# A gate product in which four of eight token groups are taken as two pairs, with seven block products for eight

## The reference

```python
x = x + xattn(layernorm(x), ctx, Wq, Wkv)     # one head, softmax over 128 context rows
x = x + ffn(layernorm(x), w_gate, w_up, w_down)

def ffn(x, w_gate, w_up, w_down):             # w_gate, w_up: (1536, 512); w_down: (512, 1536)
    x = act_qdq(x)                            # 16 bit: round(x / scale) * scale, scale = max|x| / 32767
    up = act_qdq(x @ lpbq_dequant(w_up).T)    # weights: 4 bit in blocks of 32
    gate = act_qdq(x @ lpbq_dequant(w_gate).T)
    sig = fixed_qdq_u16(sigmoid(gate))
    gate = act_qdq(gate * sig)
    o = act_qdq(gate * up)
    return o @ lpbq_dequant(w_down).T
```

## Time and profile before

| | us |
|---|---|
| median of 3 runs | 903.09 (899.49 to 903.94) |
| span of the profiled execution | 898.3 |
| gate matmuls (L871), 1152 | 250.5 |
| up matmuls (L903), 1152 | 249.0 |
| TensorE busy | 865.5 |
| VectorE busy | 651.1 |
| ScalarE busy | 560.2 |
| GpSimd busy | 157.4 |

### The profile page before, as it was taken

The page is one execution under the profiler, slowest core; times in us unless marked ns, Lnnn a source line. Parts: engine busy times, 40 slices in busy tenths (PEclk is TensorE's granted clock), DMA queues, the critical chain, the costliest instruction groups (busy, mean ns, idle before and its releaser), DMA issues.

```text
span 898.3 us, 11791 instructions
## 1 busy us (share of the span) xinstructions
PE 865.5 (96%) x4144; PEld 426.7 (47%) x4144; DVE 651.1 (72%) x918; ACT 560.2 (62%) x673; POOL 157.4 (18%) x160
## 2 busy tenths in 40 slices
PE   7999969999999999999999989999799989999998
PEld 5777544444444444444444434444344434444443
DVE  4879883754346243279997859856999997999892
ACT  2378875553553454489997859763789975555430
POOL 0099940089001950000000000000000000000000
PEclk9999989999999999999999999999999999999999
DMA  9822319775369649884339993799998897989872
GB/s 347 332 93 98 128 59 305 205 194 198 140 234 296 206 161 294 322 319 157 132 149 327 363 347 142 251 402 373 374 379 265 276 322 271 386 286 406 317 294 100
DMA packets 107548, 230.20 MB, mean 256 GB/s; under 512 B 47216, under 2 KB 47216, under 8 KB 105328
## 3 DMA queue, kind: packets, MB, share of 16 engines
q1 hardware_dynamic: 106352, 225.48, 70.8%
q10 hardware_dynamic: 1152, 4.19, 1.3%
HBM read 127.40 MB, written 92.27 MB: 245 GB/s over the span
## 4 chain that ended last, share of the span: by engine, by line
PE 66%; DVE 16%; issue 8%; DMA 6%; ACT 3%; SPq 0%; POOL 0%; DVEq 0%; ACTq 0%
PE ps L871 28%; PE ps L948 13%; PE ps L903 10%; PE ps L975 3%; DVE big L1596 3%; PE ps L804 3%; DVE big L1589 3%; PE ps L743 2%; PE ps L818 2%; DVE small L1523 2%; DMA big<-gate_park 2%; DMA product_park<-big 2%; DVE small L1511 2%; DVE big L1518 1%; PE ps L965 1%
## 5 line engine op out<-in xcount | busy, mean ns | idle before, releaser
L993 ACT ACTIVATE big<-ps 128x1024 f32<-128x1024 f32 (+2 forms) x166 | 138.7, 845 | 189.6 <-PE ps L871 102.8
L871 PE MATMUL ps<-big 128*128 (+1 forms) x1152 | 250.5, 381 | 2.3 <-DVE big L1460 2.3
L903 PE MATMUL ps<-big 128*128 (+1 forms) x1152 | 249.0, 379 | 2.3 <-ACT big L993 2.3
L871 PEld LDWEIGHTS ps<-big 128*128 128x128 f16 x1152 | 113.1, 98 | 139.4 <-issue 4.6
L903 PEld LDWEIGHTS ps<-big 128*128 128x128 f16 x1152 | 112.6, 98 | 138.5 <-issue 2.8
L1478 DVE TENSOR_REDUCE small<-big 128x1 f32<-128x1024 f32 x48 | 58.3, 1219 | 135.2 <-ACT big L993 135.1
L948 PE MATMUL ps<-big 128*128 128x512 f16 x576 | 125.1, 379 | 2.7 <-DVE big L1617 2.7
L683 POOL PARTITION_ALL_REDUCE small<-small x8 | 3.3, 410 | 509.3 <-DVE small L1558 181.5
L948 PEld LDWEIGHTS ps<-big 128*128 128x128 f16 x576 | 56.2, 98 | 71.1 <-issue 2.9
L929 PE MATMUL ps<-big 128*128 128x512 f16 x384 | 85.2, 383 | 4.5 <-ACT big L1223 4.5
L1529 DVE CUSTOM_DVE_ANT_0 big<-big,small 128x1024 f32<-128x1024 int16 x48 | 61.7, 1284 | 7.3 <-ACT big L1173 0.5
(11 more groups left out here) (101 smaller groups left out, 1008.9 us busy)
## 6 DMA issues: line engine op xcount, KB each, us to landing
big<-up_park SPq DMA_DIRECT2D x90, 512.0 KB, 6.5
up_park<-big SPq DMA_DIRECT2D x48, 512.0 KB, 3.9
gate_park<-big SPq DMA_DIRECT2D x42, 512.0 KB, 2.9
big<-gate_park SPq DMA_DIRECT2D x42, 512.0 KB, 5.7
sign_park<-big SPq DMA_DIRECT2D x48, 256.0 KB, 3.1
big<-in_x_dram SPq DMA_DIRECT2D x8, 1024.0 KB, 17.5
x_park<-big SPq DMA_DIRECT2D x8, 1024.0 KB, 3.9
product_park<-big SPq DMA_DIRECT2D x16, 512.0 KB, 5.8
```

The lines of the kernel that those rows point to most:

```text
L871: mm = nc.tensor.matmul(ps[:, 2 * (n % 2) + j], w[:, a, k, o:o + P], XT[:, g, b, k], start=(k == 0 and a + b == 0), stop=(k == KC - 1 and ...
L903: mm = nc.tensor.matmul(ps[:, b + j], WU[:, a, k, o:o + P], XT[:, g, c, k], start=(k == 0 and a + c == 0), stop=(k == KC - 1 and c == 1))
L993: return nc.scalar.activation(dst, src, ACT.Copy)
```

## The change

Groups 0 to 3 are computed as before (`flat_unit`, 24 units). Groups 4 to 7 become two pairs, (6, 7) first and (4, 5) second. For a pair and one of the six channel positions (a *quad*, 12 of them) there are two token groups, two blocks of channels and two halves of the inner dimension, a 2 x 2 by 2 x 2 block product. It is done with seven block products of six matmuls, where eight would be the plain way. TensorE runs them in the order P1, P5, P4, P6, P3, P2 of the next quad, P7: the seven calls of `six` and `first_of` in `quad` below. For that

- four sums of weight blocks (`SUMS`) are made once: GpSimd adds (`first_sums`, `last_sum`, ten operations of 1536 columns), ScalarE and VectorE split them (`sum_hi`, `sum_lo`) at units 8, 10, 13 and 16; the gate weights are scaled to 256 in place of 2048 at the top, so that the sums fit;
- four sums of token blocks per pair (`turns`) are made by VectorE from the turned integers of h, and split (`turn_raw`, `turn_hi`, `turn_lo`) at units 11 to 13 for pair (4, 5) and 17 to 19 for pair (6, 7);
- the seven products go into four banks, of which two sets alternate; ScalarE copies partial results out (`copy_out`), VectorE combines them into four halves of 512 columns (`combine`), takes their maxima (`half_max`), ScalarE their signs (`half_sign`), and SP stores each half and its signs.

Around it: the turns of h for groups 6 and 7 move to units 13 to 16 and their splits to units 15 and 17. The down weights are now first: loaded at the start of the stage, split at units 14, 16, 18 and 19 (three `natural_hi` on ScalarE and three `natural_lo` on VectorE each; `natural_hi` of a chunk waits for `natural_lo` of the chunk two before, since its output lies over inputs already used), turned at units 15, 17, 19 and 21 through a single buffer and stored one unit later each (`turn_down_weights` waits for the split and for the parking before, `park_down_weights` for its turns). The up weights are loaded in four parts at units 22 and 23, their block maxima stand on VectorE behind unit 23 and in quad 0, and they are split in quads 5 to 8 and turned in quads 7 to 10. All 48 gate tiles are now stored and fetched again; the fetches of tiles 1 to 7 are issued behind the last product, those of 8 to 22 beside the first eight up units. `WD` has another order of its dimensions.

The diff, cut to its core:

```diff
-WTOP = 2048.0
+WTOP = (256.0, 2048.0, 2048.0)
+FLAT_G = 4
+FLAT = FLAT_G * UPG
+PAIRS = (NG - FLAT_G) // 2
+QUADS = PAIRS * UPG
+SUM_AT = (8, 10, 13, 16)
+SPLIT_AT = (3, 5, 7, 9, 11, 15, 17)
+DOWN_AT = (14, 16, 18, 19)
+TURN_AT = (18, 12)
+UP_AT = (5, 6, 7, 8)
...
+            for u in range(FLAT):
+                sp.wait_ge(g_ev, u + 1)
+                sp.dma_start(gate_d[u], gate_out[:, u % 2]).then_inc(g_st[u % 2], 16)
+                sp.wait_ge(sign_ev, u + 1)
+                sp.dma_start(sign_d[u], sign_out[:, u % 2]).then_inc(sign_st[u % 2], 16)
+                if u < 10:
+                    turn_half(u)
+                if 13 <= u < 17:
+                    turn_half(u - 3)
+                if u in (15, 17, 19, 21):
+                    turn_down_weights((u - 15) // 2)
+                if u in (16, 18, 20, 22):
+                    park_down_weights((u - 16) // 2)
+                if u == 22:
+                    load_up_weights(0)
+                    load_up_weights(1)
+                if u == 23:
+                    load_up_weights(2)
+                    load_up_weights(3)
...
+            def quad(q):
+                base, pr, n = 4 * ((q + 1) % 2), q // UPG, q % UPG
+                g, T = pair_group(pr), turns(pr)
+                need(pe, c_ev, C_EV + 4 * (q - 1) if q > 1 else 0)
...
+                six(base, n, WG[:, 0], XT[:, g, :, 0:2], True)
...
+                six(base + 3, n, SUMS[:, 0], T[:, 0], True)
+                six(base + 2, n, WG[:, 2], T[:, 3], True)
+                pe.wait_ge(c_ev, C_EV + 4 * q + 1)
+                six(base, n, SUMS[:, 1], T[:, 2], False)
+                pe.wait_ge(copy_ev, COPY_EV + 4 * q + 2)
+                six(base + 3, n, SUMS[:, 2], XT[:, g + 1, :, 2:4], False)
...
+                if q + 1 < QUADS:
+                    first_of(q + 1, 4 - base)
+                pe.wait_ge(copy_ev, COPY_EV + 4 * q + 4)
+                six(base, n, SUMS[:, 3], T[:, 1], False)
...
+            for u in range(FLAT):
+                act.wait_ge(g_mm, u + 1)
...
+                if u in SUM_AT:
+                    sum_hi(SUM_AT.index(u))
+                for pr in range(PAIRS):
+                    for j in range(4):
+                        if u == TURN_AT[pr] + j // 2:
+                            turn_hi(pr, j)
+                for c in range(OC):
+                    if u == DOWN_AT[c // 3]:
+                        natural_hi(2, c)
+                act.wait_ge(g_ev, u + 1)
...
+                nc.scalar.activation(sign_out[:, u % 2], gate_out[:, u % 2], ACT.Sign).then_inc(sign_ev, 1)
...
+                if u in SPLIT_AT:
...
+                    split_h(g)
...
+                if u in SUM_AT:
+                    sum_lo(SUM_AT.index(u))
+                for pr in range(PAIRS):
+                    if u == TURN_AT[pr] - 1:
+                        turn_raw(pr, 0)
+                        turn_raw(pr, 1)
+                    if u == TURN_AT[pr]:
+                        turn_lo(pr, 0)
+                        turn_lo(pr, 1)
+                        turn_raw(pr, 2)
+                        turn_raw(pr, 3)
+                    if u == TURN_AT[pr] + 1:
+                        turn_lo(pr, 2)
+                        turn_lo(pr, 3)
+                for c in range(OC):
+                    if u == DOWN_AT[c // 3]:
+                        natural_lo(2, c)
+                if u == FLAT - 1:
+                    up_block_max(0)
+                    up_block_max(1)
...
+            for q in range(QUADS):
+                base = 4 * ((q + 1) % 2)
+                if q:
+                    last_halves(q - 1)
...
+                combine(q, 0, base, copy_b, ALU.add)
+                if q:
+                    half_max(q - 1, 2)
+                    half_max(q - 1, 3)
...
+                if q == 0:
+                    up_block_max(2)
+                    up_block_max(3)
+                    block_scales(1)
...
+                half_max(q, 0)
...
+                combine(q, 1, base + 3, copy_u, ALU.add)
+                half_max(q, 1)
```

More of the change, by code:

```diff
@@ L468, in _ @@
[L468 to L479 removed]
+                                 transpose=True).then_inc(h_turn[g % 2], 16)
@@ L892, in _ @@
             gate(0)
-            with nc.tensor.Fori(1, NG) as g:
+            with nc.tensor.Fori(1, FLAT_G) as g:
                 gate(g)
-            pe.wait_ge(wu_turned, 16 * (2 * KC + H_ODD))
+            for g in range(FLAT_G, NG):
+                pe.wait_ge(hlo_d, g + KC)
+            first_of(0, 4)
+            for q in range(QUADS):
+                quad(q)
+            pe.wait_ge(wu_turned, 16 * 2 * KC)
             def raise_unit(g, n):
@@ L1140, in _ @@
[L1140 to L1147 removed]
+            for u in range(FLAT):
+                act.wait_ge(g_mm, u + 1)
+                need(act, g_mx, u - 1)
+                if u >= 2:
+                    act.wait_ge(g_st[u % 2], 16 * (u // 2))
+                copy(gate_out[:, u % 2], ps[:, 2 * (u % 2):2 * (u % 2) + 2].rearrange("p b w -> p (b w)")).then_inc(g_ev, 1)
+                if u % 2 and u < 2 * NG - 3:
+                    h_int((u + 3) // 2)
+                if u in SUM_AT:
[8 more added lines that the diff above has]
+                act.wait_ge(g_ev, u + 1)
+                if u >= 2:
+                    act.wait_ge(sign_st[u % 2], 16 * (u // 2))
+                else:
+                    act.wait_ge(hq_d, KC + 1)
+                nc.scalar.activation(sign_out[:, u % 2], gate_out[:, u % 2], ACT.Sign).then_inc(sign_ev, 1)
@@ new lines, in copy_out, with half_sign @@
+            def copy_out(dst, bank, scale=1.0):
+                nc.scalar.activation(dst, ps[:, bank], ACT.Copy, scale=scale).then_inc(copy_ev, 1)
+            def half_sign(q, x):
+                act.wait_ge(c_ev, C_EV + 4 * q + x + 1)
+                if q:
+                    act.wait_ge(cs_st[x], CS_ST + 16 * q)
+                else:
+                    act.wait_ge(sign_st[x // 2], 16 * FLAT // 2)
+                nc.scalar.activation(sign_half[:, x], gate_half[:, x], ACT.Sign).then_inc(c_sign, 1)
@@ L1471, in _ @@
             scalar2(col["fg"], col["xs"], col["pw0"], 1.0)
-            def gate_max(g, turned=None, units=range(UPG)):
-                for n in units:
-                    dve.wait_ge(g_ev, g * UPG + n + 1)
-                    kept = isinstance(g, int) and g * UPG + n >= STAY
-                    nc.vector.tensor_reduce(gcol[:, bass.ds(g * UPG + n, 1)], shelf[:, SHELF[n]] if kept else gate_out[:, n % 2],
-                                            AX.X, ALU.max, apply_absolute_value=True).then_inc(g_mx, 1)
-                    u = g * UPG + n if isinstance(g, int) else NU
-                    if u % 2 and 3 <= u < 2 * NG:
-                        split_h(u // 2)
-                    if turned is not None:
-                        for c in (range(2 * n, 2 * n + 2) if turned == 1 else range(3 * n, min(3 * n + 3, OC))):
-                            natural_lo(turned, c)
```

569 lines of the change are left out of this document (377 added, 192 removed).

## The result

| | before | after |
|---|---|---|
| median of the runs, us | 903.24 (899.49 to 903.94) | 920.23 (918.46 to 921.12) |
| span of the profiled execution, us | 898.3 | 918.8 |
| gate stage (first gate matmul to first up matmul), us | 250.3 | 266.2 |
| up stage, us | 251.3 | 255.3 |

The ratio is 1.0188, with a 95% interval of 1.0162 to 1.0213: slower, by 17.0 us where +7.3 had been forecast, and just above the range. The profiled spans differ by 20.5 us: 15.9 in the gate stage, 4.0 in the up stage, 0.6 behind it.

A forecast was written before the change was run, and what follows sets the result against it. TensorE was taken to bound the gate stage, its matmuls back to back. The terms -15.6 + 4.1 + 1.7 + 13.5 + 3.1 + 0.5 = +7.3 us on 903.1 gave 910.4 us, range 896 to 918.

The forecast's parts named there:

- Matmuls saved: Gate stage: 72 matmuls fewer at 0.2163 us each, -15.6 us.
- the quads' pace: Quads 2 to 11: no waits, one quad being 42 matmuls at 0.2163 us, 9.1 us of TensorE.
- Rival (c): Quads 2 to 11: P6 or P7 waits 1 us in each, giving 920 us; chance 0.10.
- Sums of weights on GpSimd: Flat units: ten additions, 30 us on idle GpSimd; down-weight quantisation ends at 89 us, before it is needed; no cost.
- Sums of tokens: Flat units 11 to 19: VectorE's added work delays ScalarE's copies, so TensorE waits 4.1 and 1.7 us before units 21 and 22.
- the walk: Step-by-step timing of VectorE, ScalarE and SP from the end of unit 16, giving waits of 4.1 and 1.7 us.
- The load of up weights: First two quads: combines stand behind block maxima that wait for late loads, +13.5 and +3.1 us.
- rows of 512 bytes: Up-weight load: full rate taken; at half the rate the first two quads' waits would be 16 + 6 us.
- TensorE's clock: After the first quad's long wait a few products might run at half pace: taken as 0, up to 2 us.
- Range and up stage: After the last gate matmul two combines and two maxima replace a copy and a max: +0.5 us, passed on by the up stage.
- the twelve further tile transfers: First third of the up stage: 48 gate tiles parked and fetched for 42, costing 0, up to 2 us.
- Rival (a): Flat units and first quads: waits stay within the buffers, loads issue as the last flat unit ends, 893 us; chance 0.20.

The follow-up runs named there:

- the run with the last pair's sums later: Changed kernel with only the token sums of pair (6, 7) moved from units 17 to 19 to units 20 to 22: 912.0 us.
- the spread kernel: Changed kernel with GpSimd's last weight sum earlier, down-weight halves, pair (6, 7) sums and up-weight loads later: 902.4 us; with most GpSimd rounding cut, 897.3 us.

## Why the prediction was wrong

The direction held and the size did not. Term by term, forecast against measured, in the order of its sum:

- *Matmuls saved*: right; the quads' pace held, with no idle in quads 2 to 11. Rival (c) falls.
- *Sums of weights on GpSimd, "free"*: this step failed. Not that anyone waits for GpSimd, nobody does. Its rounding was to begin 40 us into the stage and end at 89, and went from 54 to 111 (183.65 to 241.2 us). It began late because the last weight sum stands ahead of it, which begins 7 us after the maximum over partitions (before has the same gap of 6.8 us) and takes 10.6 us; and its 32 operations took 57.5 us for the 48.6 of the forecast (the multiplication by the inverse scale 1826 ns for the 1521 of the earlier trace rows). And for all that time it stretches VectorE's two-tensor work. Cover was looked for in whether the engine was free; the cost lay in what it does to its neighbour.

```profile
165.76 0.38 POOL L796 PARTITION_ALL_REDUCE small<-small  x1 [8.59 <-DVE small L1546]
173.03 6.61 POOL L817 TENSOR_TENSOR big<-big 128x1536 f32<-128x1536 f16 x2 [6.89 <-issue]
179.72 3.97 POOL L844 TENSOR_TENSOR big<-big 128x1536 f32<-128x1536 f32 x1
183.65 3.00 POOL L805 TENSOR_TENSOR big<-big,small 128x768 f32<-128x768 f32 x1
```

- *Sums of tokens*: +5.8 forecast before units 21 and 22; 6.0 measured before unit 21, released by ScalarE's copy as forecast. That the sizes agree is partly luck: with GpSimd's rounding thinned out, at the durations that the walk had used, 3.3 us were left there. And 6.7 us came before units 16, 17 and 19, which the walk did not have. It set out with VectorE on time at the end of unit 16 and took GpSimd as "done by then", so it priced nothing beside a working GpSimd, although by its own forecast GpSimd worked up to unit 16; it worked into unit 19. VectorE was late by then: the split of group 6, which the walk ends 1.4 us after unit 16, ended 10.8 us after it (230.7 against 219.9). The first pair's sums at units 11 to 13, which the walk leaves out, stand ahead of it.
- *The load of up weights*: +13.5 and +3.1 forecast, 11.1 and 1.0 measured, at the place and behind the maxima that were named; the load was issued 4.7 us after the last flat matmul and not 8. Right in mechanism, 4.4 us too large. What was missed is that the same loads hold the parks, which shows only once the maxima are out of the way. As for rows of 512 bytes, on which the bound hung: the four loads landed 8.2 us after issue at the median, while other transfers shared the queues, so no run here prices such rows by themselves.
- *TensorE's clock*: forecast 0, up to 2; measured about 7 in the gate stage and 1.7 in the up stage. This step failed too, and it is the largest single term missed. It was judged by one gap of 2.3 us; behind a gap of 3.4 us, and behind those of 6 and 11, matmuls ran 2 to 3 us long. The trace of before had a second gap of 2.3 us, the one ahead of its gate stage, which follows some microseconds of small matmuls, and behind that one the clock was 0.50 (132 to 134 us, above).
- *Range and up stage*: +0.5 forecast, +4.0 measured: wait 4.6 for 2.3 us, and 1.7 at half clock. The range itself was on time (the first gate product 9.98 us after the stage's start, before 9.73) and the 27th product stands at 94.16 us in both. Only the thirteen behind it, where VectorE waits up to 7.7 us for a load of gate tiles, fall back, by 2.3 us at the 40th. In the other kernels it is 0 to 2.6. The prediction's term for this is the twelve further tile transfers, which it put at 0, up to 2; no run takes them away, so why these loads land later stays open.

So the difference of 13.2 us between forecast and spans is +6.7 (early flat waits) + 0.2 - 4.4 (load) + 7.2 (clock) + 3.5 (up stage), with the rest of -0.6 (before's own 1.2 us at half clock, less 0.6 of modelled ends) and +0.6 behind the up stage. Rival (a) had VectorE and ScalarE half idle as its support; that was true of before, and at the durations of before.

**What the trace of before had shown.** The stretching stands there too, in a line that the earlier trace rows gave as a mean of 1604 ns (L1469, the low half of the split). Its single instances, from VectorE's timeline; GpSimd begins to quantise at 183.05 us there:

```profile
180.05 1.22 DVE L1469 TENSOR_TENSOR big<-big 128x2048 f16<-128x2048 int16 x1
...
186.94 2.38 DVE L1469 TENSOR_TENSOR big<-big 128x2048 f16<-128x2048 int16 x1
...
197.10 1.73 DVE L1469 TENSOR_TENSOR big<-big 128x2048 f16<-128x2048 int16 x1
```

1.22 us ahead of GpSimd's work and 1.7 to 2.4 beside it: a mean over both hid a factor of two. And the durations that the prediction took as the price of two-tensor work (0.683, 1.220, 1.279) are all from quiet stretches: the natural low parts of before lie between 232 and 343 us and never beside GpSimd. The Trainium skill ("SBUF — State Buffer", section Who interferes with whom) has the rule: a VectorE instruction with two SBUF inputs contends with a GpSimd instruction that reads SBUF, and one with at most one SBUF input, outside the modes that use two ports, doesn't. The rows above agree, 1.2 to 2.46 us for a difference and 1.21 for the maximum. Whether the stretched cast (last section) falls under that condition no run here shows.

## What to carry to other kernels

Before work is put on an idle GpSimd, look at what VectorE does beside it: with two SBUF inputs an instruction took 1.2 to 3.3 times its quiet duration here, and a mean over a line's instances hides it, so read single instances inside and outside GpSimd's busy time. A burst of loads in a queue is paid twice, by those who wait for the data and by the stores behind it; take one away and the other shows. Every idle gap that a change adds to TensorE may bring a slower clock behind it (2.2 to 2.7 us were lost behind each of the three longest in the gate stage), so a wait of several microseconds can cost more than its length.

## What the runs showed of the hardware that was not expected

- VectorE beside GpSimd: 1.22 to 2.46 us (differences of 1024 int16 columns), 1.28 to 2.0 (low parts), 0.65 to 1.6 (low parts of 512 columns), 1.22 to 4.01 (the low half of a split beside the last weight sum), while a maximum over 1024 columns stayed at 1.21. A cast from int16 (L1707), which reads one tensor, also went from 0.69 to 1.75.
- A gap's price in clock varied: behind 3.36 us of idle before unit 17, 48 matmuls took 13.27 us in the changed kernel and 10.53 in the run with the last pair's sums later, behind the same 3.36 us. Behind 2.05 us in the spread kernel with less GpSimd work, 42 took 10.90 for 9.24, and behind 1.92 us in the changed kernel nothing was lost.
